# VectorE's order in the feed-forward step: four operations moved between others

## The reference

```python
x = x + 0.5 * _L0_ffn_ref(_layernorm(x), w_gate, w_up, w_down)
x = x + _L0_attn_ref(_layernorm(x), Wqkv, bqkv, Wout, bout, gamma, beta)
x = x + 0.5 * _L0_ffn_ref(_layernorm(x), w_gate, w_up, w_down)
```

```python
scale = max(max(abs(block)) / 6.0, 1e-12)
q = GRID[searchsorted(MID, abs(block / scale))] * sign(block) * scale
gate, y = linear(x, w_gate), linear(x, w_up)
out = linear(silu(gate) * y, w_down)
```

## Time and profile before

| | us |
|---|---|
| median of three runs | 2226.59 |
| the profiled execution | 2225.92 |
| its span, first to last instruction | 2224.2 |
| TensorE busy (matmul) | 2124.0, 95% of the span |
| VectorE busy | 2066.5, 93% |
| ScalarE busy | 1915.0, 86% |
| GpSimd busy | 1897.5, 85% |

### The profile page before, as it was taken

The page is one execution under the profiler, slowest core; times in us unless marked ns, Lnnn a source line. Parts: engine busy times, 40 slices in busy tenths (PEclk is TensorE's granted clock), DMA queues, the critical chain, the costliest instruction groups (busy, mean ns, idle before and its releaser), DMA issues.

```text
span 2224.2 us, 91039 instructions
## 1 busy us (share of the span) xinstructions
PE 2124.0 (95%) x30384; PEld 1496.2 (67%) x30384; DVE 2066.5 (93%) x5231; ACT 1915.0 (86%) x4136; POOL 1897.5 (85%) x3002
## 2 busy tenths in 40 slices
PE   3899999999999899999999999979999999999998
PEld 1566666666666688888888888855666665666565
DVE  7999999999999689999999999978999999999997
ACT  7888888888888789999999999978888888888885
POOL 6899999999999678888888888868989999989996
PEclk9999999999999999999999999999999999999999
DMA  4765555555556432222222222224655555555555
GB/s 104 128 121 115 116 113 112 115 116 114 114 112 109 75 56 60 60 59 59 59 59 58 60 59 58 60 47 79 114 112 112 112 112 112 112 112 113 112 117 117
DMA packets 719856, 208.74 MB, mean 94 GB/s; under 512 B 666400, under 2 KB 719520, under 8 KB 719776
## 3 DMA queue, kind: packets, MB, share of 16 engines
q1 hardware_dynamic: 719776, 207.76, 46.5%
HBM read 20.38 MB, written 16.78 MB: 17 GB/s over the span
## 4 chain that ended last, share of the span: by engine, by line
DVE 41%; PE 25%; issue 13%; POOL 12%; DMA 4%; DVEq 2%; SPq 2%; ACT 1%; POOLq 0%; ACTq 0%
DVE ffn_y L748 10%; DVE ffn_per_block L717 9%; DVE ffn_hx L710 7%; PE ffn_ps_gu L860 6%; PE attn_ps_qk L1260 5%; DVE ffn_q L744 3%; PE ffn_ps_down L872 3%; DMA attn_xT<-attn_x_hl 3%; POOL ffn_h_hl L791 3%; POOL ffn_h_hl L790 3%; PE attn_ps_num L1300 3%; PE attn_ps_v_second L1276 2%; PE attn_ps_sc L1313 2%; DVE ffn_scale L723 2%; SPq L1033 2%
## 5 line engine op out<-in xcount | busy, mean ns | idle before, releaser
L860 PE MATMUL ffn_ps_gu<-wgu_hi,ffn_xT 128*128 128x512 f16 (+1 forms) x3072 | 739.0, 363 | 16.2 <-DVE ffn_hx L710 7.5
L860 PEld LDWEIGHTS ffn_ps_gu<-wgu_hi,ffn_xT 128*128 128x128 f16 x3072 | 300.9, 98 | 302.6 <-issue 21.7
L806 ACT ACTIVATE ffn_quarter<-ffn_y,offsets 128x960 int16<-128x960 f32 (+2 forms) x264 | 282.6, 1071 | 185.2 <-DVE ffn_y L748 185.2
L860 PE MATMUL ffn_ps_gu<-wgu_lo,ffn_xT 128*128 128x512 f16 (+1 forms) x1536 | 431.5, 363 | 0.0
L872 PE MATMUL ffn_ps_down<-wd_hi,ffn_hT 128*128 128x256 f16 x2816 | 349.9, 273 | 18.8 <-DVE x_sb L737 12.7
L790 POOL TENSOR_TENSOR ffn_h_hl<-ffn_q,ffn_h_scale_hi 128x704 f16<-128x704 f16 x256 | 352.2, 1376 | 12.5 <-DVE ffn_h_scale_lo L754 8.5
L791 POOL TENSOR_TENSOR ffn_h_hl<-ffn_q,ffn_h_scale_lo 128x704 f16<-128x704 f16 x256 | 354.0, 1383 | 0.0
L872 PEld LDWEIGHTS ffn_ps_down<-wd_hi,ffn_hT 128*128 128x128 f16 x2816 | 265.1, 98 | 99.0 <-issue 35.5
L717 DVE TENSOR_REDUCE ffn_per_block<-ffn_hx 128x60 f32<-128x960 f32 (+2 forms) x264 | 298.4, 1130 | 21.3
L748 DVE TENSOR_TENSOR ffn_y<-ffn_hx,ffn_per_block 128x960 f32<-128x960 f32 (+2 forms) x264 | 294.8, 1117 | 0.0
L842 ACT ACTIVATE ffn_odd<-ffn_quarter,offsets 128x960 f16<-128x960 int16 (+2 forms) x264 | 278.7, 1056 | 10.8 <-POOL ffn_shift L783 10.8
(11 more groups left out here) (184 smaller groups left out, 5177.6 us busy)
## 6 DMA issues: line engine op xcount, KB each, us to landing
x_sb<-in_L_attn_x SPq DMA_DIRECT2D x128, 128.0 KB, 2.4
out<-x_sb SPq DMA_DIRECT2D x128, 128.0 KB, 2.1
attn_v_eo<-attn_v_nat SPq DMA_DIRECT2D x256, 34.0 KB, 1.8
ffn_xT<-ffn_x_hl SPq DMA_TRANSPOSE x256, 2.4
ffn_hT<-ffn_h_hl SPq DMA_TRANSPOSE x256, 3.5
attn_xT<-attn_x_hl SPq DMA_TRANSPOSE x128, 2.4
attn_oT<-attn_o_hl SPq DMA_TRANSPOSE x128, 2.5
x_sb<-in_L_ffn_w_gate SPq DMA_DIRECT2D x2, 352.0 KB, 5.2
```

The source lines that it names most:

```text
L806: nc.scalar.activation(quarter[:, back], y[:, back], ACT.Identity, bias=offsets[:, 0:1], scale=4.0 / HALF_MIN).then_inc(S["quarter"], 1)
L860: last = nc.tensor.matmul(ps_gu[par][:, a:b], xT[par][:, c, :], w[:, k, a:b], start=(n == 0), stop=(n == len(terms) - 1))
```

## The change

Four operations of VectorE move; none is added or taken away, and each keeps its waits. Lines 751 and 754 (`x_scale_lo` and `h_scale_lo`) stood behind line 748. Now `x_scale_lo` of a tile is made one step later, between lines 710 and 717, and `h_scale_lo` of the same tile as before between lines 717 and 723. The addition to x (line 737) stands between 723 and 726. `h_pow2` (line 758) stands between 744 and 748, and 761 stays behind 748. No operation now reads what the one directly ahead of it wrote.

```diff
--- before.py
+++ after.py
@@ -708,6 +708,10 @@
                 ready(dve, "up_done", th)
                 ready(dve, "silu", th)
                 nc.vector.scalar_tensor_tensor(hx[par][:, 0:INNER], ps_gu[par][:, INNER:2 * INNER], unscale[:, 1:2], silu[:], ALU.mult, ALU.mult).then_inc(S["h"], 1)
+            if valid(tx - 1, N):
+
+                ready(dve, "x_scale_hi", tx - 1)
+                nc.vector.tensor_tensor(x_scale_lo[oth][:], scale[oth][:, HB:], x_scale_hi[oth][:], ALU.subtract).then_inc(S["x_scale_lo"], 1)
             if front:
 
                 if valid(th, N):
@@ -715,12 +719,20 @@
                 if valid(tx, N):
                     ready(dve, "xn", tx)
                 nc.vector.tensor_reduce(amax[:, blocks_in(front)], blocks(hx[par][:, front]), AXX, ALU.max, apply_absolute_value=True).then_inc(S["amax"], 1)
+            if valid(th - 1, N):
+                ready(dve, "h_scale_hi", th - 1)
+                nc.vector.scalar_tensor_tensor(h_scale_lo[oth][:], scale[oth][:, 0:HB], h_rpow2[oth][:], h_scale_hi[oth][:], ALU.mult, ALU.subtract).then_inc(S["h_scale_lo"], 1)
             if front:
                 round_ready(dve, "amax", i)
                 if valid(th, N):
                     freed(dve, "h_scale_hi", th, 2)
                 at = blocks_in(front)
                 nc.vector.tensor_scalar(scale[par][:, at], amax[:, at], 1.0 / (6.0 * HALF_MIN), MIN_SCALE / HALF_MIN, ALU.mult, ALU.max).then_inc(S["scale"], 1)
+            if valid(ta, N):
+
+                ready(dve, "down_done", ta)
+                ready(dve, "h_unscale", ta)
+                nc.vector.scalar_tensor_tensor(x_sb[:, ta, :], ps_down[:, 0:D], column(h_unscale, ta), x_sb[:, ta, :], ALU.mult, ALU.add).then_inc(S["added"], 1)
             if front:
                 round_ready(dve, "scale", i)
                 nc.vector.reciprocal(inv[:, at], scale[par][:, at]).then_inc(S["inv"], 1)
@@ -730,11 +742,6 @@
             if valid(th, N):
 
                 nc.vector.tensor_reduce(h_top[:], scale[par][:, 0:HB], AXX, ALU.max).then_inc(S["h_top"], 1)
-            if valid(ta, N):
-
-                ready(dve, "down_done", ta)
-                ready(dve, "h_unscale", ta)
-                nc.vector.scalar_tensor_tensor(x_sb[:, ta, :], ps_down[:, 0:D], column(h_unscale, ta), x_sb[:, ta, :], ALU.mult, ALU.add).then_inc(S["added"], 1)
             if back:
                 round_ready(dve, "odd", i - 1)
                 if valid(th - 1, N):
@@ -742,20 +749,14 @@
                 if valid(tx - 1, N):
                     freed(dve, "x_split", tx - 1, 2)
                 nc.vector.tensor_scalar(q[oth][:, back].bitcast(I16), odd[:, back].bitcast(I16), TO_CODE, TO_CODE, ALU.add, ALU.subtract).then_inc(S["q"], 1)
+            if valid(th, N):
+                ready(dve, "h_top", th)
+                freed(dve, "h_unscale", th, 2)
+                nc.vector.tensor_scalar(h_pow2[par][:].bitcast(I32), h_top[:].bitcast(I32), EXP_MASK, None, ALU.bitwise_and).then_inc(S["h_pow2"], 1)
             if front:
                 round_ready(dve, "inv", i)
                 round_freed(dve, "quarter", i, 1)
                 nc.vector.tensor_tensor(blocks(y[:, front]), blocks(hx[par][:, front]), over_block(inv[:, at], at.stop - at.start), ALU.mult).then_inc(S["y"], 1)
-            if valid(tx, N):
-                ready(dve, "x_scale_hi", tx)
-                nc.vector.tensor_tensor(x_scale_lo[par][:], scale[par][:, HB:], x_scale_hi[par][:], ALU.subtract).then_inc(S["x_scale_lo"], 1)
-            if valid(th - 1, N):
-                ready(dve, "h_scale_hi", th - 1)
-                nc.vector.scalar_tensor_tensor(h_scale_lo[oth][:], scale[oth][:, 0:HB], h_rpow2[oth][:], h_scale_hi[oth][:], ALU.mult, ALU.subtract).then_inc(S["h_scale_lo"], 1)
-            if valid(th, N):
-                ready(dve, "h_top", th)
-                freed(dve, "h_unscale", th, 2)
-                nc.vector.tensor_scalar(h_pow2[par][:].bitcast(I32), h_top[:].bitcast(I32), EXP_MASK, None, ALU.bitwise_and).then_inc(S["h_pow2"], 1)
             if valid(th, N):
                 ready(dve, "h_pow2", th)
                 nc.vector.tensor_scalar(h_rpow2[par][:].bitcast(I32), h_pow2[par][:].bitcast(I32), -1.0, RPOW2_BITS, ALU.mult, ALU.add).then_inc(S["h_rpow2"], 1)
```

## The result

The changed kernel took **2341.29 us** (median of 4 runs, 2335.92 to 2343.80) against 2226.87 us before (median of 4). The ratio is 1.0511, with a 95% interval of 1.0498 to 1.0525. Its profiled execution took 2335.92 us, with a span of 2334.2 us.

What follows compares the result with a forecast made beforehand. TensorE (5.42 us a step) and VectorE (5.39) were taken as nearly equal bounds; collisions with GpSimd would make VectorE's step 5.97. Over 240 steps that adds 116 us to 2225.9; with 0.7 for the median, 2343 us, range 2275 to 2380.

Steps and rivals of the forecast that it cites:

- The bound and the cap: Stages A and B: VectorE 5.39 us a step, TensorE 5.42; TensorE's pace caps any gain at some 16 us.
- The order's own saving: VectorE's step in the new order: vanished stalls save 0.44 us, 5.39 to 4.95, without collisions.
- The collision and its arithmetic: Moved x_scale_lo and h_scale_lo wait for the ends of GpSimd's lines 790 and 791; step becomes 5.97 us.
- Who asks first goes first: Between two gapless GpSimd operations, waiting VectorE gets in first: x_scale_lo ends 0.03 us after line 790, at 3.57.
- rival 2: x_scale_lo held behind both GpSimd lines 790 and 791: 7.19 us a step, +409 us, about 2635 us; chance 0.07.
- The sum: Both stages: 240 x 5.97 = 1432.8 us against 1316.8, +116 us; steps outside counted zero, within 10 us.
- GpSimd's phase renews itself: GpSimd's round, 5.53 us at most, is below 5.97, so it waits for q at every step.
- Rivals 1 and 3: Stages: no collision, -16 us, chance 0.12; or collisions in some steps or one stage, +51 us, chance 0.10.
- Rival 1's price: No collision in the stages: TensorE bounds every step at 5.42 us, -16 us, 2210 us; chance 0.12.
- The loop's turn: VectorE's loss of some 0.4 us ahead of line 710 at the turn costs nothing more.
- the case by rows 5 and 6 alone: Each moved scale operation waits at most 0.24 us: step 5.43 us, a gain of some 15 us.

Runs made afterwards that it cites:

- e7: e4 with the variance's epsilon added by VectorE behind the addition to x instead of by GpSimd: 2211.44 us.
- e10: As e7, but the first 12 tiles keep GpSimd's own addition of the epsilon: 2204.48 us, ratio 0.9902 to the kernel before.
- e4: Changed kernel, with the block scales also written to PSUM and read there by x_scale_lo and h_scale_lo: 2219.64 us.
- e3: Changed kernel with both x_scale_lo and h_scale_lo back behind y; the addition to x and h_pow2 keep their new places: 2225.68 us.
- e2: Changed kernel with h_scale_lo alone back behind y: 2320.87 us.
- e1: Changed kernel with x_scale_lo alone back behind y, where it stood before: 2337.05 us.
- e5: Kernel before, with x_scale_lo alone computed from the block maxima in PSUM, the scale's floor left out: 2229.17 us.
- e6: Changed kernel with x_scale_lo one operation later, behind the reduction and directly ahead of h_scale_lo: 2369.99 us.
- e11: e3 with VectorE adding the variance's epsilon for GpSimd, except in the first 12 tiles: 2206.97 us.

## Why the prediction was right

- **The bound and the cap.** TensorE had 5.42 us a step and VectorE 5.39. With all else out of the way, in e7 and e10, the stages take 5.40 to 5.41 us a step. So the cap of 16 us was worked out a little low: the stages of e10 are 19.1 us shorter than those of the kernel before (1297.7 against 1316.8 us), and its whole time is 20.4 us shorter.
- **The order's own saving** was right: with the collisions taken out in e4, VectorE follows TensorE at 5.42 in stage A and idles 0.31 us of it in the step shown. That leaves 5.11 us for its own work, where 4.95 + 0.14 = 5.09 had been worked out for e4. In the changed kernel the distances are 1.06 us from the reduction to h_scale_lo (1.08 taken) and 0.14 from scale to the addition.
- **The collision and its arithmetic.** Predicted from q on: 2.39 and 3.57 for start and end of x_scale_lo, 3.49, 4.57, 4.94 and 4.86 for the reduction, h_scale_lo, its end and scale, 5.97 for the next q. Measured in the step shown: 2.36, 3.63, 3.56, 4.62, 5.01, 4.93 and 6.02. The excess of 0.05 is the parity of GpSimd's start (0.61 instead of 0.53); the other half of the steps has 5.93. The mean is 5.98 in A and 5.94 in B.
- **Who asks first goes first** decided between +116 and +409 us. The row of the changed kernel bears it out: 714 ended at 434.16 while 792, started at 434.09, ran until 435.48. Nor does rival 2 show anywhere: it would hold line 714 for about 2.5 us, and the longest of its 110 records above has 1.286, the longest of all 256 in the run 1.620.
- **The sum.** +116 us forecast, 2341.29 - 2226.87 = 114.4 measured. Stage A gave 62.3 for 61.0, stage B 51.4 for 55.0 and the rest -3.7 for 0 within 10. These add up to the 110.0 us between the two profiled executions, and that of the changed kernel was the fastest of its four. So each term was right within 4 us; that the medians come within 2 us of the forecast is in part luck.
- **GpSimd's phase renews itself**: between 80 and 600 us it idles before every one of the 87 operations of line 782. The profile puts 57 of these waits down to q. The other 30, among them the 0.91 us of the step shown, it puts down to GpSimd's own line 774; but that had ended 0.9 us earlier, and 782 starts 0.22 us behind the end of q, so I read them as the same wait. Rivals 1 and 3 never set in within the stages. The margin was small, though: x_scale_lo came 0.12 us or more behind the start of line 791 in stage A and in some steps of stage B only 0.08.

What was wrong lies in the parts that did not set the time. **Rival 1's price** (2210 us if nothing collides) took TensorE for the only bound that is left. In e3 (2225.7) and e4 (2219.6) neither scale operation meets a long one, and they still miss it: in stage B GpSimd's own round and its meeting with q take 5.53 us. I had the round as 5.53 at most in the prediction and used it only to show that GpSimd is back in time, not to ask whether it is above 5.42. **The loop's turn** is not quite free: the steps across it take 6.08 us in A and 6.16 in B instead of 6.02 and 5.97. And **the case by rows 5 and 6 alone**, 5.43 us a step, was put at a gain of some 15 us; 240 x 5.43 = 1303.2 makes it 13.6.

That VectorE's two scale operations cost by their two SBUF inputs is shown (e4). That the order of asking decides between two GpSimd operations is shown in rows of three kernels (before, changed, e2), but no run varied the time of asking by less than 0.1 us around a boundary, so how near a tie is won stays open.

## What to carry to other kernels

An operation that is moved to fill a stall must be looked up in the other engines' timelines at its new place, not at its old one. With two SBUF inputs it can wait there until GpSimd's instruction ends (here 1.27 us instead of 0.17), and two such waits in a step did not add up: either alone cost nearly as much as both (e1, e2). Taking one operation out of a collision can push its neighbour, or the other engine, into it (e5). Ask what bounds next before pricing the case in which all goes well (e3, e4).

## What was not expected of the hardware

- q, with one input, collides in both directions. It held GpSimd's one-column operation for up to 0.2 us (0.402 instead of 0.189, e5) and was itself held for 0.4 us (0.817 instead of 0.40, e4, stage B).
- A one-column operation of GpSimd did not hold VectorE up: in the kernel before, x_scale_lo started at 428.49 inside the operation below and ran at its 0.17 us, while operations of 256 columns cost it up to 0.24 us.

```profile
428.34 0.26 POOL L783 TENSOR_SCALAR ffn_shift<-ffn_neg_mean,ffn_rstd 128x1 f32<-128x1 f32 x1
```

- Line 710 takes 0.934 us in the changed kernel, e1, e3 and e6, where it took 0.951 before and again in e5 and e7 to e11, with nothing altered about it. In e4 it takes 0.952 us in stage A and 0.934 in stage B of one and the same execution. So it goes with what runs beside it. I have no explanation, and no run was made for it.
